# A four-stage graph kernel: 24 of the 197 tail tiles and 8 dense units moved from the last stage into hop three

## What is computed

```python
def reference(x, src, dst, edge_weight, shared_weight, output_bias):   # x 100000 x 256, 25000 edges, dst sorted
    def _spmm(edge_src, edge_dst, edge_weight, feats, n_nodes):
        msgs = edge_weight[:, None] * feats[edge_src]
        return jax.ops.segment_sum(msgs, edge_dst, num_segments=n_nodes)
    feats, cur = [x], x
    for _ in range(3):                       # three hops
        cur = _spmm(src, dst, edge_weight, cur, 100000)
        feats.append(cur)
    y = jnp.concatenate(feats, axis=1) @ shared_weight + output_bias
    return _layernorm(x + y, axis=-1)
```

## Time and profile before

| what | value |
|---|---|
| timed runs | 1563.0, 1560.13, 1560.88 us; median 1560.88 |
| profiled execution | span 1564.9 us (the page gives no other time for it) |
| PE busy | 1431.5 us, 91% |
| DVE busy | 1207.2 us, 77% |
| ACT busy | 1077.5 us, 69% |
| POOL busy | 1070.6 us, 68% |
| DMA | 410.75 MB, mean 262 GB/s |
| mean granted clock of PE | 0.974 |
| hop three | about 811 to 982 us |
| stage D | about 1004 to 1565 us |

### The profile page before, as it was taken

One profiled execution on the slowest core, in us unless ns is written; L12 is line 12 of the kernel. 1 busy time (PEld: TensorE's weight loads), 2 busy tenths in 40 slices (PEclk: granted clock), 3 DMA queues, 4 the chain that ended last, 5 costly groups with the idle time before them and its releaser, 6 DMA issues. The chain is left out here.

```text
span 1564.9 us, 31198 instructions
## 1 busy us (share of the span) xinstructions
PE 1431.5 (91%) x7990; PEld 1202.6 (77%) x7990; DVE 1207.2 (77%) x4961; ACT 1077.5 (69%) x2674; POOL 1070.6 (68%) x1043
## 2 busy tenths in 40 slices
PE   7999999999999986699979999998889888899993
PEld 5888888888888865588868887777767776677882
DVE  6877777777777778978744443699999999999773
ACT  4777777777777743368855454577777878778774
POOL 4577777777777754657736666457777777777764
PEclk9999999999999988799989999999999999999996
DMA  7888888888888874389966676799999999999862
GB/s 241 272 272 271 265 286 281 279 273 270 278 279 281 273 209 151 96 288 330 318 210 171 149 163 149 229 302 330 324 339 327 333 325 328 336 335 328 299 219 92
DMA packets 214326, 410.75 MB, mean 262 GB/s; under 512 B 30996, under 2 KB 137485, under 8 KB 214154
## 3 DMA queue, kind: packets, MB, share of 16 engines
q1 hardware_dynamic: 164534, 311.03, 58.8%
q0 software_dynamic: 48624, 97.04, 22.4%
q10 hardware_dynamic: 996, 0.72, 0.2%
HBM read 227.02 MB, written 194.09 MB: 269 GB/s over the span
## 5 line engine op out<-in xcount | busy, mean ns | idle before, releaser
L1381 PE MATMUL ps_y<-w_sb,xT 128*128 128x256 f32 x2640 | 701.3, 391 | 28.4 <-DVE y_ring L1719 14.8
L1381 PEld LDWEIGHTS ps_y<-w_sb,xT 128*128 128x128 f32 x2640 | 474.7, 195 | 96.5 <-ACT xT L1098 27.9
L1111 ACT ACTIVATE o_ring<-y_ring,shift,rstd 128x256 f32<-128x256 f32 (+1 forms) x782 | 422.3, 590 | 0.0
L1719 DVE TENSOR_TENSOR y_ring<-ps_y,bias 128x512 f32<-128x512 f32 x391 | 268.6, 687 | 134.1 <-PE ps_y L1381 118.4
L1725 DVE BATCH_NORM_STATS2 stats<-y_ring 128x6 f32<-128x256 f32 (+1 forms) x782 | 291.0, 414 | 3.7
L849 POOL DMA_INDIRECT rows_in<-in_x,gather_idx x200 | 201.3, 1006 | 87.0 <-issue 63.6
L849 POOL DMA_INDIRECT tails_found<-tail_keys,table_idx x200 | 200.2, 1001 | 81.4 <-issue 58.5
L853 POOL DMA_INDIRECT out_rows<-u_out,tailo_idx x197 | 203.7, 1034 | 74.1 <-issue 47.0
L849 POOL DMA_INDIRECT rows_in<-out_rows,tailx_idx x160 | 167.9, 1049 | 81.5 <-issue 40.5
L1465 PE MATMUL ps_u<-w_sb,cT 128*128 128x256 f32 x788 | 206.2, 384 | 0.0
L1370 PE MATMUL ps_xT<-ident,x_ring 128*128 128x128 f32 x1196 | 186.2, 279 | 12.8 <-ACT xT L1098 6.6
(11 more groups left out here) (320 smaller groups left out, 2268.8 us busy)
## 6 DMA issues: line engine op xcount, KB each, us to landing
x_ring<-in_x SPq DMA_DIRECT2D x195, 512.0 KB, 6.6
out_rows<-o_ring SPq DMA_DIRECT2D x195, 512.0 KB
c_rows<-sums SPq DMA_DIRECT2D x49, 512.0 KB
u_rows<-u_out SPq DMA_DIRECT2D x49, 512.0 KB
keys_bc<-u_rows SPq DMA_DIRECT2D x25, 512.0 KB, 7.2
tails_found<-u_rows SPq DMA_DIRECT2D x12, 512.0 KB, 7.2
listed<-u_rows SPq DMA_DIRECT2D x12, 512.0 KB, 6.5
c_list_rows<-sums SPq DMA_DIRECT2D x11, 512.0 KB
```

What stands on the lines that cost most here:

```text
L1111: last = act.activation(o_ring[slot][0:rows, r * D:(r + 1) * D], y_ring[k][0:rows, r * D:(r + 1) * D], ACT.Identity, bias=shift[k][0:rows, ...
L1381: last = pe.matmul(ps_y[p % 2][0:rows, r * D:(r + 1) * D], columns_of(p)[0][:, q * P:q * P + rows], w_sb[:, c, :], start=c == 0, stop=c == ...
L1719: dve.tensor_tensor(y_ring[k][0:rows, half * 2 * D:(half + 1) * 2 * D], ps_y[half][0:rows, :], bias2[0:rows, :], ALU.add).then_inc(y_copie ...
```

## The change

Quads (groups of four tail tiles) 0 to 5 are fixed up in hop three, in groups 2 to 9, and stage D starts with step 3. Groups 2 to 9 of hop three have two dense units instead of one (8 units more); stage D has 21 steps, all of 4 units (84 units; before 24 steps with 92). POOL's list for tile n becomes `gather_c(n)`, `gather_early`, `scatter_early` of the tile eight places back, `scatter_v(n - 4)`: the gathers stand in groups 2 to 7, the scatters in groups 4 to 9. All sums of the hop go to bank `ps_sum[0]`, and the other holds the spread deviations. The index copies `tailx_idx` and `tailo_idx` are gone: gathers and scatters take their index from `early_node` and `tail_node` themselves. The first split of the deviations moves from `bridge_d` to `bridge_c`. Tiles whose rows are not ready in time are to go to the serial loop at the end, as before (`landed_limit` is a new condition for that).

```diff
-    D_UNIT = C_UNIT + ONE * FIRST_GROUPS + FOUR
+    E_GROUP = 2
+    E_QUADS = 6
+    E_STEPS = E_QUADS * G // Q
+    EARLY = Q * E_STEPS
+    C_SIZES = (ONE,) * E_GROUP + (PAIR,) * (FIRST_GROUPS - E_GROUP)
+    D_UNIT = C_UNIT + sum(C_SIZES) + FOUR
-    D_SIZES = (FOUR,) * KEPT_STEPS + (STEP,) * (D_STEPS - KEPT_STEPS)
+    D_SIZES = (0,) * E_STEPS + (FOUR,) * (D_STEPS - E_STEPS)
...
+            def gather_early(i):
+                d, q, j = i // Q, i % Q, i // G
+                until(pool, cy_copied, i - G + 1)
+                rows = UROWS * early_window(j)[1]
+                limit(rows)
+                gather(rows_in[G + i % G][:, :], out[0:rows, :], early_node[:, i:i + 1], tailx_in[q])
+            def scatter_early(i):
+                pool.wait_ge(cnormed, i + 1)
+                limit(N)
+                scatter(out[:, :], eo[i % Q], early_node[:, i:i + 1], scattered[i % Q // 2])
             def group_c(g):
                 for k in range(G):
                     n = G * g + k
                     gather_c(n, k)
+                    if isinstance(g, int):
+                        i = G * (g - E_GROUP) + k
+                        if 0 <= i < EARLY:
+                            gather_early(i)
+                        if 0 <= i - 2 * G < EARLY:
+                            scatter_early(i - 2 * G)
                     if not isinstance(g, int) or g > 0:
                         scatter_v(n - G, k)
...
-                copy_sum(C_TILE + n, k % 2, k)
+                copy_sum(C_TILE + n, 0, k)
...
+            def early_roots(j):
+                act.wait_ge(cvar_ready, j + 1)
+                act.activation(cstd[j % 2][:, :], cmv[j % 2][:, :, 1], ACT.Sqrt, bias=eps[:, :]).then_inc(cstd_ready, 1)
+            def early_normalise(i):
+                q, j, k = i % Q, i // G, i % G
+                act.wait_ge(cshift_ready, j + 1)
+                until(act, scattered[q // 2], 32 * (i // Q))
+                act.activation(eo[q], ey[q], ACT.Identity, bias=cshift[j % 2][:, k:k + 1],
+                               scale=crstd[j % 2][:, k:k + 1]).then_inc(cnormed, 1)
             for n in range(G * FIRST_GROUPS):
...
                     carry_c((n + 1) // G, (n + 1) % G)
                 dense_slot(c_step(g), 2 * k + 1)
                 copy_t(n, k)
+                j = g - E_GROUP - 1
+                if k == 1 and 0 <= j < E_QUADS:
+                    early_roots(j)
+                if k == 3 and 0 <= j < E_QUADS:
+                    for i in range(2):
+                        early_normalise(G * j + i)
+                if k == 0 and 0 <= j - 1 < E_QUADS:
+                    for i in range(2, G):
+                        early_normalise(G * (j - 1) + i)
...
-                    sum_tile(C_TILE + n, k % 2, k, k)
+                    sum_tile(C_TILE + n, 0, k, k)
...
+                    if isinstance(g, int) and k == G - 1 and 0 <= g + 1 - E_GROUP < E_QUADS:
+                        spread_early(g + 1 - E_GROUP)
+            def spread_early(j):
+                pe.wait_ge(parts_hot, j + 1)
+                pe.wait_ge(std_split, 1 + 4)
...
+                if 0 <= g - E_GROUP < E_QUADS:
+                    load_early_u(g - E_GROUP)
...
                 dense_slot(c_step(g), 2 * k)
+                if k == 0 and 0 <= j < E_QUADS:
+                    sum_early(j)
+                if 0 <= i < EARLY:
+                    early_stats(i)
...
-                        columns(tailx_idx[1 - par][:, :], early_node if d + 1 < KEPT_STEPS else tail_node, Q * d + Q, Q).then_inc(tailx_staged, 1)
...
-                        columns(tailo_idx[1 - par][:, :], early_node, Q * d - Q, Q).then_inc(tailo_staged, 1)
```

More of the change, by code:

```diff
@@ L93, in gnn_program @@
     assert 3 * SPLIT_COLS <= Q * SLOTS
-    assert all(kept_window(d)[1] <= (D_OFFS[d - 1] if d > 0 else D_UNIT - FOUR) - STEP for d in range(KEPT_STEPS))
+    assert all(kept_window(d)[1] <= (D_OFFS[d - 1] if d > E_STEPS else D_UNIT - FOUR) - STEP for d in range(E_STEPS, KEPT_STEPS))
     AHEAD0 = REAL - Q
@@ L240, in gnn_program @@
         begun_before = sb("begun_before", [P, 2])
-        tailx_idx = [sb(f"tailx_idx{k}", [P, Q], i32) for k in range(2)]
-        tailo_idx = [sb(f"tailo_idx{k}", [P, Q], i32) for k in range(2)]
+        landed_limit = sb("landed_limit", [P, EARLY])
         ahead_idx = sb("ahead_idx", [P, Q], i32)
@@ L279, in gnn_program @@
         picked_out = sels[:, :, :].rearrange("p k c -> p (k c)")[:, 0:Q * WCOLS]
+        ey = [t[:, G * P + h * D:G * P + (h + 1) * D] for t in keys_bc for h in range(2)] + [sums[:, G + k, :] for k in range(G)]
+        eo = [t[:, :] for t in (signs, source_key, not_padding, segment_in, key_in, w1, own_T, tail_f)]
+        eu_even = listed[:, :, :].rearrange("p t f -> p (t f)")[:, 0:G * D]
+        eu = [[eu_even[:, k * D:(k + 1) * D] for k in range(G)], [cT[k // 2][:, k % 2 * D:(k % 2 + 1) * D] for k in range(G)]]
+        e_picked = part_f[:, 0:G * WCOLS]
         ps_xT = pb("ps_xT")
@@ L293, in gnn_program @@
         ps_std = (ps_u[0], ps_u[1])
+        ps_early = ps_sum[1][:, 0:G * WCOLS]
         ps_t = ps_u[0]
@@ L486, in each_d_step @@
         def each_d_step(run):
-            for d in range(D_STEPS):
+            for d in range(E_STEPS, D_STEPS):
                 run(d, d_step(d), d % 2, d // 2)
@@ L730, in _ @@
                 group_c(g)
-            load_ahead(c_step(FIRST_GROUPS - 1), 0)
+            for k in range(C_SIZES[-1]):
+                load_ahead(c_step(FIRST_GROUPS - 1), k)
             with sp.Fori(FIRST_GROUPS, n_groups) as g:
@@ L780, in step_d @@
                     load_ahead(dense, 3)
-            for g in range(4):
-                load_u(g, g)
+            for g in range(2 * E_STEPS, 2 * E_STEPS + 4):
+                load_u(g, g % 4)
             for k in (2, 3):
@@ L981, in scatter_v, with await_stores @@
                                         compute_op=ALU.add).then_inc(v_scattered[k], 16)
+            def await_stores(first, end):
+                for u in range(first, end):
+                    pool.wait_ge(stored[u % RING], 16 * (u // RING) + 16)
+                    limit(N)
[7 more added lines that the diff above has]
+                pool.wait_ge(cnormed, i + 1)
+                limit(N)
+                scatter(out[:, :], eo[i % Q], early_node[:, i:i + 1], scattered[i % Q // 2])
             def group_c(g):
@@ L993, in _ @@
                 limit(CROWS)
-            group_c(0)
-            with pool.Fori(1, n_groups) as g:
+            pool.wait_ge(late_ready, 1)
+            limit(CROWS)
+            await_stores(early_window(E_QUADS - 1)[1] - RING, early_window(E_QUADS - 1)[1])
+            for g in range(FIRST_GROUPS):
+                group_c(g)
+            with pool.Fori(FIRST_GROUPS, n_groups) as g:
                 group_c(g)
@@ L1010, in gather_d @@
                 limit(rows)
-                gather(rows_in[q][:, :], out[0:rows, :] if n < KEPT else x[:, :], tailx_idx[par][:, q:q + 1], tailx_in[q])
+                index = (early_node if n < KEPT else tail_node)[:, n:n + 1]
+                gather(rows_in[q][:, :], out[0:rows, :] if n < KEPT else x[:, :], index, tailx_in[q])
             def scatter_d(n, q, d, par):
-                if q == 0:
-                    pool.wait_ge(tailo_staged, d + 1)
-                    limit(N)
                 pool.wait_ge(cnormed, n + 1)
                 limit(N)
-                scatter(out[:, :], co[q], tailo_idx[par][:, q:q + 1], scattered[q // 2])
-            def await_stores(first, end):
-                for u in range(first, end):
-                    pool.wait_ge(stored[u % RING], 16 * (u // RING) + 16)
-                    limit(N)
+                scatter(out[:, :], co[q], early_node[:, n:n + 1], scattered[q // 2])
             def step_d(d, dense, par, turn):
@@ L1605, in group_c @@
                     turn_rows(ps_t, (own_c2[k], sums[:, k, :]), t_psum)
+                    if isinstance(g, int) and k == G - 1 and 0 <= g + 1 - E_GROUP < E_QUADS:
[3 more added lines that the diff above has]
+                pe.wait_ge(std_split, 1 + 4)
+                until(pe, std_picked, j)
+                first, end = early_window(j)
+                cols = RPP * (end - first)
+                for k in range(G):
+                    q = G * (j % 2) + k
+                    for m, part in enumerate(std_parts):
+                        last = pe.matmul(ps_early[:, WCOLS * k:WCOLS * k + cols], part_hot[:, q * P:(q + 1) * P],
+                                         part[:, RPP * first:RPP * end], start=m == 0, stop=m == 2)
+                    last.then_inc(std_spread, 1)
             for g in range(FIRST_GROUPS):
```

244 lines of the change are left out of this document (164 added, 80 removed).

## The result

The changed kernel takes **1594.12 us** (median of 4 runs, 1589.7 to 1595.62) against 1561.94 for the kernel before on the same chip: ratio 1.0199, 95% interval 1.018 to 1.0218, slower by 32 us. The forecast was 1582 with a range of 1552 to 1602. The profiled execution's span is 1592.1 us, 27.2 more than before. Executions that fell into a second state of the chip, some per cent longer at a lower granted clock, are left out of the medians and ratios of this document.

What follows compares the result with a forecast made beforehand. TensorE was taken to bound hop three and VectorE stage D's kept steps, GpSimd close behind. Hop three 74 us more, stage D 53 less: 21 slower on 1560.9, giving 1582 us, range 1552 to 1602.

Steps and rivals of the forecast that it cites:

- the held queue: Hop three, groups 4 to 9: GpSimd's first early scatter waits for ScalarE's normalised tile, delaying the next gather; 74 us more; chance 0.52.
- L: Hop three: landing time of a group's first gather, taken as 4.4 us from stage D's 2.8 least and 5.9 median.
- The fixed part: Hop three, first gather of a group to the second, beyond landing: 2.6 us ScalarE and signals, scatter 1.32, `scatter_v` 1.89; 5.8 us.
- Stage D: All parts of that stage together: 65.3 + 2.4 + 2.6 - 17.3 = 53.0 us less, held firm to about 4 us.
- The kept steps: Stage D, first pick to last: VectorE sets the step at 21.78 us; three steps go, 65.3 us less.
- the index copies: Stage D: copies go from 17 steps, displacing about 0.14 us a step, 2.4 us less.
- The four last steps: End of stage D: 4 units instead of 3, TensorE full, each step 4.33 us more, 17.3 us.
- the stretch up to the first pick: Before stage D's first pick: moving the first split of the deviations forward removes TensorE's stall at the first spread, 2.6 us less.
- Full queue only: Rival, hop three: GpSimd only full, normalised tile there in time; hop 47.7 us more, 5 us faster in all, 1556; chance 0.17.
- TensorE sets the hop: Rival: TensorE sets hop three throughout; 37.3 us more there, 53.0 less in stage D, 1545 us; chance 0.10.
- Clock lost too: Rival, hop three: TensorE drops to its lower clock after each of six waits; 18 us on top, 1600; chance 0.18, with landings over 6 us.

Runs made afterwards that it cites:

- the wait alone: Early scatters ten tiles behind their gathers, but GpSimd's wait for the normalised tile left at the changed kernel's place, eight behind: 1591.3 us, ratio 1.0192.
- the later scatter: Changed kernel with each early scatter issued ten tiles behind its gather instead of eight, the last two after the tenth group: 1548.7 us, ratio 0.9915.

## Why the prediction was right, and where it was off

**The mechanism** is as forecast, and shown: the held queue, by the wait alone (42.6 us) and by the later scatter (45.4). Of the signs named ahead, four DMAs a tile without free time, one wait a group ended by ScalarE, TensorE at about 75% in the hop (78), steps of 21.6 us (21.67) and last steps of 26 are there. Groups 4 to 7 were to last 26 to 30 us: from hold to hold they took 30.1, 32.4, 31.1 and 29.5, three of four above that range (the next took 26.5). Groups 2 and 3, said to take about 20, took 18.9 and 18.3 on GpSimd, from first gather to first gather. The wait itself was to be 2 to 5 us and is 6.7 to 8.8.

**The term that was mis-sized is L**, the landing time: "I take 4.4, midway between the least and the median", with the sentence ahead of it: "The trace has no gather at this place, so L is bounded by stage D's". It had one that was nearer. The earlier trace rows holds a hop gather issued at 856.33 us and the earlier trace rows its carry at 862.75, after a wait of 2.48 us for that very DMA: 6.4 us. The same pair is there in eight further groups of the kernel before, 6.3 to 8.1 us. It is the group's second tile and not its first, but it comes right behind SyncE's transfers, as the first does in the changed kernel. The gathers of tile 0 took 5.2 to 7.9 us in the changed kernel, mean 6.3. With 6.4 for L the six groups cost 12 us more, and the sum is 1594. That this is the measured time is luck, as the next paragraph shows.

**From the span to the time.** Of the 12 us between 1582 and 1594 only half lies in the stretches: the span grew by 27.2 us where 21 was forecast; the hop came out 15.2 us longer than forecast and the other stretches together 9.1 us shorter. The other 6 us come from "the median of the timed runs is 4.0 us below that span". In each of the changed kernel's executions the time is 1.8 to 1.9 us above the span, so the profiled execution before, at 1564.9 us, was itself some 6 us longer than the median one (an estimate), and the 4.0 was a difference between two executions. Nothing shows which of its stretches was the longer for it.

**The fixed part** of the hold was 5.8 us and is 6.5 in the four groups where it can be read best (from the gather of tile 0 to that of tile 1: 12.6, 14.3, 13.4 and 11.7, less L). What was short is the signal: 0.1 us was taken, and from the end of the first normalised tile (941.72) to the scatter are 0.9. (The profile puts the wait down to the second normalised tile, which ended at 942.21; the code waits for the first only.) The fixed part is thus 0.7 us longer a group, 3 us in four. The three tiles behind the hold take 17.8 us (17.64 forecast).

Groups 4 to 7 thus last 123.0 us against 111.4: 8.3 us of the excess is L, 2.9 the fixed part, 0.4 the tiles. The forecast for the other four groups and the hop's end was 4 us short; the first hold of group 4, with GpSimd's lead of two tiles, is in there.

**One landing too few.** The prediction's chain began at the gather of tile 0. The normalised tile also stands behind tile 3's carry, and when tile 0 is made to land sooner, tile 3 sets the time, by way of TensorE's turned rows. In the run with the table rows earlier that is what the timeline at the turn to group 6 shows; that it is also what left 22 of 48 us of waits when ScalarE normalised ahead of the carry fits the order, and was not tried apart.

**Stage D** was forecast at -53.0 us and came to -58.2. The kept steps and the index copies are right to 0.6 us. The four last steps cost 26.0 us each as forecast (from 21.7), but after the last pick only 12.7 of the 17.3 us show. The four steps did give theirs: from the first to the last product of the tail tiles it is 111.4 us against 94.5, 16.9 more. What follows the last of these products is 21.6 us against 26.0; the reason for that was not looked into. The stretch up to the first pick is 3.8 us shorter where 2.6 was taken.

**The start of the hop** was forecast at nothing. The hop comes 3.9 us sooner; the first sum waits 1.50 us where it waited 4.55, here on TensorE's timeline, and the clock there is 1.00 where it was 0.86.

```profile
810.73 0.69 PE L1509 MATMUL ps_sum<-rows_in,sels 128*128 128x256 f32 x2 [1.50 <-DVE sels L2045]
```

The split of the deviations moved into the bridge ahead of it, and the wait for GpSimd's first gathers is shorter; which of the two gave the 3.9 us was not tried.

**The rivals.** Full queue only, 1556, 5 us faster: this is the kernel once the wait is moved, 1548.7, 13 us faster. TensorE sets the hop: not reached, even then it is at 92%. Clock lost too: the clock was lost, the time was not; its 18 us counted TensorE's work as on the path, where the path of the changed kernel runs through the landings, ScalarE and GpSimd. The best of the full-queue case was computed at 47.7 us for the hop, and the repaired hop takes 43.1 more than before.

## What to carry to other kernels

When a step is moved into a stage, its wait counts by what stands behind it on the same queue: here a scatter that nobody was waiting for stood ahead of a gather that everybody waited for, and issuing it two tiles later turned 2% slower into 0.9% faster. The price of such a hold is a landing time at that very place, so look for any pair of issue and release there (a carry that waits for its gather) before borrowing a number from another stage. And a lower clock or an idle engine can be a mark of the wait and not a cost on top of it; here it was.

## What the runs showed of the hardware that was not expected

- The same gather of 128 rows takes 2.6 us from issue to carry when it goes out right after a hold, and 4.2 to 8.2 us at the turn of a group, among SyncE's transfers. Taking most of the bytes out of the loads there brought tile 0 down to 2.5 to 3.7 us and tile 3 only to 4.9 to 6.6.
- After 5.42 us of idleness two records of TensorE took 1.19 us and the eight after them 2.90; with waits of this kind once or twice a group the granted clock is 0.90 over 121 us. Filling them with matmuls brings it to 1.00 and changes the length of that stretch by 0.3 us.
- One chip ran the kernel before 17 and 19% slower than the other, and the version with ten tiles' lag 18%, with hop three nearly unchanged (146.3 us with one bank against 146.9). In the other stages its engines waited for several us at a time; the cause stays open, and the changed kernel itself was not run there.
